# Six places instead of four for attention's exponentials, and a narrower layout of V

## The chip, the cores and the metric

The kernel runs on one core of a Trainium2 chip. The time is the device time of one execution in microseconds; the lower the better. Several executions are taken and their median is compared.

## The reference

The program is one forward pass over `x` of 2 sequences, 1024 tokens and width 128, in six residual steps: a small feed-forward, attention, the same feed-forward, a mixture of experts, a bidirectional Mamba block, the mixture of experts again. Each reads a layer norm of `x`. The change is in attention alone:

```python
qkv = x @ W_qkv.T + b_qkv            # 16 heads of 8
q, k = rope(q), rope(k)
scores = einsum('bhqd,bhkd->bhqk', q, k) / sqrt(8)
w = softmax(scores)                  # over 1024 keys
out = einsum('bhqk,bhkd->bhqd', w, v)
x = x + out
```

## The kernel before, in words

Everything stays in SBUF, and each stage is one program per engine, ordered by hand with semaphores. The first stage, `ffn_and_attention` (L747), runs the first feed-forward, attention, and, woven between attention's steps, the second feed-forward and the routing of the experts for both sequences. It ends near 325 us of the span. All engines meet at the end of its block (L763), and `moe_mamba_moe` follows.

Attention is cut into 16 blocks (`BLOCKS`, L648), eight per sequence. A block is one head of each group of four heads (`m`) and one half of the queries (512). A block has 16 steps (`UNITS`), one for each of 8 key tiles of 128 and each of 2 pairs of heads; step `w` of the 256 does:

- `scores` (L656), TensorE: two matmuls (one per head of the pair) of 128 keys by 512 queries into one of three PSUM places (`SB` = 3, each 128x1024 f32). In blocks 0 and 1 they are f32 with 32 rows (L677); from block 2 on, bf16 with 64 rows (L680), the f32 operands being split into bf16 parts and laid side by side by DMA. It waits until the exponential of step `w - 3` has freed the place.
- `exp` (L683), ScalarE: one ACTIVATE of 128x1024 from PSUM to one of `PB` = 4 places of `p` in SBUF (L687). It waits for its scores and, from step `PB` on, until the weighing of step `w - PB` has read the place (`summed`).
- `weigh` (L691), TensorE: two f32 matmuls (L703), weights V (128 keys by 32 columns), moving `p` (512 queries), into 32 rows of the PSUM bank `ps_av` for each group of heads. The 32 columns of V are: 8 values of the head, a 1 (so that the row sum of the softmax comes out of the same matmul) and zeros. For an even head the values stand at columns 0 to 7 and the 1 at 8; for an odd one at 16 to 23 and 24. So two heads one after the other can add into the same rows, each with zeros where the other's are.

The order on TensorE is written out in `ffn_and_attention` (from block 2 on), for even `w`, with `BEHIND` = 4:

```python
a.scores(pe, w)
a.weigh(pe, w - BEHIND)
a.weigh(pe, w - BEHIND + 1)
a.scores(pe, w + 1)
# then, at some steps, side work: a transpose, a projection, ...
```

In blocks 0 and 1 `scores(pe, w)` comes behind the two weighings. Side work stands after the scores of some steps: Q, K and V of the second sequence in blocks 4 and 5 (L361, L367), transposes of the norm (L1158) and of attention's output (L711), matmuls of the feed-forward (L1205, L1244) and of the routing (L1470). They use one PSUM bank in turn (`side`). When a turn of blocks closes, VectorE copies `ps_av` to `mixed` (L721), TensorE transposes it, and VectorE divides by the row sums and adds to `x` (`finish`, L714). At the first step of block 8 TensorE passes a branch on a flag (`shift_tensor`, L579), which is not taken with these inputs.

Other users of what the change touches: `fill` (L736), GpSimd, sets V to zero for one sequence (L739) and writes the ones (L743); `take_v` (L400), VectorE, adds the bias and writes V (L406); the first feed-forward (`FirstFfn`, L1256) keeps its 16 hidden values in `places`, which are the 8 halves of `p`, then the halves of `q`, `k_all` and `k`, and `rest`, all still unused at that time.

Of the kernel before, what the change touches and what calls it, by code (L numbers as in the profile page):

```python
# [16 lines left out]
P = 128  # L17
B, T, D = 2, 1024, 128
TILES = B * T // P
TPB = T // P  # L20
GROUP = 4
# [6 lines left out]
HEADS, HD = 16, 8  # L28
HG = 4
HGROUPS = HEADS // HG  # L30
# [83 lines left out]
class Core:  # L114
# [6 lines left out]
    def sb(self, name, shape, dt=F32, ctx=None):  # L121
        return (ctx or self.ctx).enter_context(self.nc.sbuf_tensor(name, shape, dt))

    def sem(self, name, ctx=None):

        s = self.nc.alloc_semaphore(name)
        if ctx is not None:
            self.stage_sems.append(s)
        return s
# [153 lines left out]
class Attention:  # L283
# [33 lines left out]
    def open(self, ctx):  # L317
        core, nc, name = self.core, self.core.nc, self.name
        sb = lambda n, shape, dt=F32: core.sb(f"{name}_{n}", shape, dt, ctx)
        sem = lambda n: core.sem(f"{name}_{n}", ctx)  # L320
        self.v = sb("v", [P, TILES, HEADS, 32])
        self.q, self.k_all, self.k = sb("q", [D, T]), sb("k_all", [D, T]), sb("k", [D, T])
        self.parts, self.rest = sb("parts", [D, 2, self.PARTS, T], BF16), sb("rest", [D, 2, GT])
        self.q_rows, self.k_rows = sb("q_rows", [P, 2, 2, T], BF16), sb("k_rows", [P, 2, 2, T], BF16)
        self.p = sb("p", [P, self.PB, 2, BANK])
        self.mixed = sb("mixed", [P, BANK])
        self.rden, self.scaled = sb("rden", [P, GROUP, HG, 2]), sb("scaled", [P, GROUP, HG, 2, HD])
        self.work = sb("work", [P, 7, GT])
        self.t_cos, self.t_sin = (self.work[:, 2 * i:2 * i + 2, :] for i in range(2))
        self.squares = self.mixed[:, 0:2 * D].rearrange("p (k d) -> p k d", k=2)  # L330
        self.b_squares, self.row_sums = sb("b_squares", [D, 2]), sb("row_sums", [D, 2])
        self.one = sb("one", [P, 1])
        self.head_sums, self.bounds, self.bound, self.flag = sb("head_sums", [1, 2 * HEADS]), sb("bounds", [1, HEADS]), sb("bound", [1, 1]), sb("flag", [1, 1], I32)
        self.top, self.minus_top = self.mixed[:, 2 * P:3 * P], self.mixed[:, 3 * P:4 * P]
        self.minus_parts = self.mixed[:, 0:2 * P].bitcast(BF16)[:, 0:self.PARTS * P].rearrange("p (j n) -> p j n", j=self.PARTS)
        self.marks_made = self.p[0:HD, 0, 0, :].bitcast(BF16)
        banks = ctx.enter_context(nc.psum_tensor(f"{name}_ps", [P, 8, BANK], F32))
        self.ps = banks
        self.ps_s, self.ps_av, self.ps_side = banks[:, 0:2 * self.SB, :].rearrange("p (s a) n -> p s a n", a=2), banks[:, 6, :], banks[:, 7:8, :]
        self.v_filled, self.masked_dve = sem("v_filled"), sem("masked_dve")  # L340
        self.qk_done, self.v_done, self.v_read, self.qk_read, self.rot_done = (sem(n) for n in ("qk_done", "v_done", "v_read", "qk_read", "rot_done"))
        self.masked_act, self.shift_in, self.stored = sem("masked_act"), sem("shift_in"), sem("stored")
        self.part0, self.rested, self.part1, self.part2 = (sem(n) for n in ("part0", "rested", "part1", "part2"))
        self.landed = [sem(f"landed{i}") for i in range(2)]
        self.squared, self.rows_summed, self.rows_done, self.heads_summed, self.heads_read, self.flagged = (
            sem(n) for n in ("squared", "rows_summed", "rows_done", "heads_summed", "heads_read", "flagged"))
        self.scored, self.exped, self.summed, self.av_read, self.turned, self.den_done, self.out_done, self.o_read = (
            sem(n) for n in ("scored", "exped", "summed", "av_read", "turned", "den_done", "out_done", "o_read"))
        of_both = {n: sem(f"shift_{n}") for n in ("turned", "negated")}
        self.shifting = [{**of_both, **{n: sem(f"shift{b}_{n}") for n in ("masked", "scored", "maxed", "own", "kept", "rows")}} for b in range(B)]  # L350
        self.registers = {}
# [48 lines left out]
    def take_v(self, dve, side, i):  # L400

        nc = self.core.nc
        dve.wait_ge(self.v_done, i + 1)
        dve.wait_ge(self.v_filled, 3 * (i // 2) + 3)
        for odd in range(2):
            ins = nc.vector.tensor_tensor(self.v[:, i * GROUP:(i + 1) * GROUP, odd::2, self.column(odd):self.column(odd) + HD],  # L406
                                          side.of(("v", i)).rearrange("p (j h d) -> p j h d", j=GROUP, h=HEADS)[:, :, odd::2, :],
                                          self.b_v[:].rearrange("p (h d) -> p h d", h=HEADS)[:, odd::2, :].unsqueeze(1).to_broadcast([P, GROUP, HEADS // 2, HD]),
                                          ALU.add)
        ins.then_inc(self.v_read, 1)  # L410

    @staticmethod
    def column(m):
        return 16 * (m % 2)

    def mask_first(self, act):
        self.core.landed(act, "head_mask")
# [220 lines left out]


    UNITS = 2 * TPB  # L640
    SB, PB = 3, 4
    BLOCKS = [(0, 0, 0, 0), (0, 0, 1, 0), (0, 1, 0, 1), (0, 1, 1, 1), (0, 2, 0, 2), (0, 3, 0, 3), (0, 2, 1, 2), (0, 3, 1, 3)]
    BLOCKS += [(1, 0, 0, 4), (1, 1, 0, 5), (1, 2, 0, 6), (1, 3, 0, 7), (1, 2, 1, 6), (1, 3, 1, 7), (1, 0, 1, 8), (1, 1, 1, 9)]
    TURNS = [(0,), (1,), (2,), (3,), (4, 5), (6, 7), (8, 9), (10, 11), (12, 13), (14, 15)]
# [46 lines left out]
    def weigh(self, pe, w):  # L691
        n, u = w // self.UNITS, w % self.UNITS
        b, m, half, _ = self.BLOCKS[n]
        kt, pair = u // 2, u % 2
        if u in (0, TPB):
            pe.wait_ge(self.v_read, 2 * b + u // TPB + 1)
        if u == 0:
            if n and self.opens(n):
                pe.wait_ge(self.av_read, self.turn_of(n))
        pe.wait_ge(self.exped, w + 1)  # L700
        for j in range(2):
            i = 2 * pair + j
            ins = self.core.nc.tensor.matmul(self.ps_av[32 * i:32 * i + 32, :], self.v[:, b * TPB + kt, HGROUPS * i + m, :],  # L703
                                             self.p[:, w % self.PB, j, :], start=(kt == 0 and self.opens(n)), stop=(kt == TPB - 1 and self.closes(n)))
        ins.then_inc(self.summed, 1)

# [29 lines left out]
    def fill(self, pool, b):  # L736

        nc, v = self.core.nc, self.v[:, b * TPB:(b + 1) * TPB, :, :]
        nc.gpsimd.memset(v, 0.0).then_inc(self.v_filled, 1)  # L739
        pool.wait_ge(self.v_filled, 3 * b + 1)  # L740
        for odd in range(2):
            one = self.column(odd) + HD
            nc.gpsimd.memset(v[:, :, odd::2, one:one + 1], 1.0).then_inc(self.v_filled, 1)  # L743
        pool.wait_ge(self.v_filled, 3 * b + 3)


# [1045 lines left out]
class Mamba:  # L1792
# [271 lines left out]
    def window(self, u, c, k):  # L2064

        di, b = self.UNITS[u]
        t0 = k if di == 0 else 2 * (TAPS - 1) - k
        return self.padded[:, c % 2, t0:t0 + T], self.taps[:, di, c, k:k + 1]
# [804 lines left out]
```

## Time and profile before

| | us |
|---|---|
| runs: 860.19, 863.32, 865.90; median | 863.32 |
| span of the profiled execution, first to last instruction | 852.2 |
| median less that span | 11.1 |
| first and last start of an exponential | 46.4, 318.6 |
| PE, ACT, DVE busy | 716.2, 543.8, 496.4 |

The page gives for the profiled execution only its span; what lies around it is taken as the 11.1 us by which the median of the runs is longer. PE is TensorE's matmuls, PEld its weight loads, ACT ScalarE, DVE VectorE, POOL GpSimd. An f32 matmul leaves two records (two passes), so one `weigh` has four and a bf16 `scores` two. Ends of matmuls are modelled: records of consecutive matmuls overlap, and the time that one takes of TensorE is read from start to start. "Idle before" of an instruction is the time in which its engine had nothing running, and behind the arrow stands what released it.

### The profile page before, as it was taken

The page shows a single profiled execution, that of the slowest core. Times are in us where ns is not written, and L with a number is a line of the kernel's source. Part 1 is how long each engine was busy: PE and PEld are TensorE (multiplying, and loading weights), DVE is VectorE, ACT ScalarE, POOL GpSimd, SP SyncE. Part 2 cuts the span into 40 slices and gives each one's busy share as a digit, 9 for nine tenths or more (in the row PEclk, how much of TensorE's full clock was granted, in tenths as well). Part 3 has the DMA queues.
Part 4 walks back from the last instruction along what each step waited for, and adds up shares of the span by engine and source line. Part 5 has one row for each costly group of instructions (what it writes and reads, how often), then busy time and mean ns, then how long its engine had stood idle before and what let it go on. Part 6 is the DMA issues. An engine that isn't in the chain of part 4 may idle for free. (4 is left out here: it accounts for less than half of the span.)

```text
span 852.2 us, 12981 instructions
## 1 busy us (share of the span) xinstructions
PE 716.2 (84%) x4016; PEld 373.4 (44%) x4016; DVE 496.4 (58%) x1453; ACT 543.8 (64%) x938; POOL 298.8 (35%) x328
## 2 busy tenths in 40 slices
PE   4799999989999997898779886778887768797995
PEld 1432222212222224565446454566566645564654
DVE  6778432204855747743437469798798847332352
ACT  5367997889998983644256684967877615342331
POOL 3090003301000434434323456444562732545342
PEclk9799999999999999999889988998999979998998
DMA  4046934521492211112212042112221311211313
GB/s 130 1 187 161 183 86 81 199 91 60 175 261 82 86 36 50 40 34 50 80 28 55 20 117 56 58 50 60 71 72 52 99 49 56 58 42 47 88 53 89
DMA packets 76410, 70.11 MB, mean 82 GB/s; under 512 B 9687, under 2 KB 60233, under 8 KB 76080
## 3 DMA queue, kind: packets, MB, share of 16 engines
q1 hardware_dynamic: 71024, 60.56, 26.6%
q0 software_dynamic: 5024, 8.54, 3.0%
q8 instruction: 36, 0.59, 0.3%
q14 instruction: 38, 0.31, 0.1%
q10 hardware_dynamic: 288, 0.10, 0.1%
HBM read 41.23 MB, written 29.02 MB: 82 GB/s over the span
## 5 line engine op out<-in xcount | busy, mean ns | idle before, releaser
L687 ACT ACTIVATE attn_p<-attn_ps 128x1024 f32<-128x1024 f32 x256 | 240.7, 1059 | 34.7 <-PE attn_ps L703 20.7
L1665 PE MATMUL ps_main<-moe_xsT,moe_w 128*128 128x320 f32 x384 | 131.0, 469 | 14.6 <-issue 9.1
L703 PE MATMUL attn_ps<-attn_p,attn_v 128*32 128x512 f32 x1024 | 137.5, 608 | 4.2 <-issue 4.0
L1675 ACT ACTIVATE moe_act_h<-ps_main 128x320 f32<-128x320 f32 (+1 forms) x128 | 55.1, 433 | 115.2 <-PE ps_main L1665 60.6
L1690 DVE TENSOR_TENSOR moe_hid<-moe_act_h,ps_main 128x320 f32<-128x320 f32 (+1 forms) x128 | 61.9, 485 | 110.8 <-ACT moe_act_h L1675 51.0
L1559 POOL DMA_INDIRECT moe_slots<-rows,moe_scatter_at x64 | 63.8, 997 | 97.8 <-DVE moe_scatter_at L1548 38.0
L680 PE MATMUL attn_ps<-attn_q_rows,attn_k_rows 64*128 64x512 bf16 x448 | 84.5, 388 | 11.5 <-ACT attn_p L687 7.7
L1665 PEld LDWEIGHTS ps_main<-moe_xsT,moe_w 128*128 128x128 f32 x384 | 70.7, 200 | 49.7 <-issue 29.5
L1695 PE MATMUL ps_main<-moe_hid,moe_w 128*128 128x320 f32 (+1 forms) x256 | 74.9, 458 | 5.1 <-DVE moe_hid L1690 3.7
L680 PEld LDWEIGHTS attn_ps<-attn_q_rows,attn_k_rows 64*128 64x128 bf16 x448 | 20.3, 93 | 134.2 <-ACT attn_p L687 119.6
L1765 POOL DMA_INDIRECT moe_rows<-moe_y,moe_dest x48 | 46.2, 962 | 78.6 <-ACT moe_y L1758 39.7
L2084 DVE SCALAR_TENSOR_TENSOR mb_act<-mb_padded,mb_taps,mb_act 128x1024 f32<-128x1024 f32 x48 | 67.1, 1407 | 2.9 <-ACT mb_act L2075 2.3
L1695 PEld LDWEIGHTS ps_main<-moe_hid,moe_w 128*128 128x128 f32 (+1 forms) x256 | 41.9, 192 | 34.7 <-issue 15.3
L1195 POOL TENSOR_TENSOR x_sb<-x_sb,bout_half 128x1024 f32<-128x1024 f32 (+1 forms) x4 | 7.3, 1837 | 104.7 <-DVE rows L1150 104.7
L2245 POOL TENSOR_TENSOR mb_z<-mb_y_in,mb_z 128x256 f32<-128x256 f32 x24 | 26.3, 1098 | 47.8 <-DVE mb_y_in L2236 33.0
L436 POOL TENSOR_SCALAR attn_parts<-attn_q 128x512 bf16<-128x512 f32 x4 | 2.5, 616 | 114.6 <-DVE attn_q L398 114.6
L2124 ACT ACTIVATE mb_e_seg<-mb_cums,mb_cum_col 128x128 f32<-128x128 f32 x128 | 40.5, 389 | 1.2 <-DMA mb_cums<-mb_cum_kept 1.2
L703 PEld LDWEIGHTS attn_ps<-attn_p,attn_v 128*32 128x32 f32 x1024 | 20.6, 108 | 42.5 <-issue 36.9
L2048 PE MATMUL ps_side<-norm_xT,mb_w_xbc 128*128 128x512 f32 x64 | 33.4, 641 | 5.5 <-DVE mb_ab L2017 5.5
L1765 POOL DMA_INDIRECT moe_rows<-mb_y,moe_dest x24 | 22.9, 955 | 38.8 <-ACT mb_y L1758 24.8
L2179 PE MATMUL ps_main<-mb_xw,mb_bs 128*128 128x256 f32 x56 | 20.0, 442 | 19.6 <-DVE mb_h L2202 12.8
L2156 DVE TENSOR_TENSOR mb_mt<-mb_e_seg,mb_gm 128x512 f32<-128x512 f32 x32 | 26.9, 840 | 15.6 <-ACT mb_e_seg L2131 9.5
(273 smaller groups left out, 1288.0 us busy)
## 6 DMA issues: line engine op xcount, KB each, us to landing
mb_cums<-mb_cum_kept SPq DMA_DIRECT2D x32, 256.0 KB
moe_slots<-zeros SPq DMA_DIRECT2D x4, 1380.0 KB, 14.0
attn_q_rows<-attn_q_parts SPq DMA_DIRECT2D x36, 128.0 KB
attn_k_rows<-attn_k_parts SPq DMA_DIRECT2D x36, 128.0 KB
moe_w<-in_w SPq DMA_DIRECT2D x3, 1536.0 KB, 11.6
moe_rows<-zeros SPq DMA_DIRECT2D x4, 1024.0 KB, 16.2
moe_back<-moe_rows SPq DMA_DIRECT2D x16, 256.0 KB, 4.0
mb_e_cum<-mb_e_cum_kept SPq DMA_DIRECT2D x56, 64.0 KB
```

Source lines behind the costliest of these rows:

```text
L680: ins = self.core.nc.tensor.matmul(into, self.k_rows[rows, ring, pair, keys], self.q_rows[rows, ring, pair, queries], start=True, stop=True)
L687: self.core.nc.scalar.activation(self.p[:, w % self.PB, :, :].rearrange("p a n -> p (a n)"), self.ps_s[:, w % self.SB, :, :].rearrange("p ...
L703: ins = self.core.nc.tensor.matmul(self.ps_av[32 * i:32 * i + 32, :], self.v[:, b * TPB + kt, HGROUPS * i + m, :], self.p[:, w % self.PB, ...
L1559: nc.gpsimd.indirect_dma_start(self.slots[r], bass.IndirectOffsetOnAxis(self.scatter_at[:, b, k, j:j + 1], 0), self.row_of[:, b * TPB + j, ...
L1665: self.core.nc.tensor.matmul(ps[:, w % 2, 0:CAP], wt[:, e, c * P:(c + 1) * P], self.xsT[:, u % 2, :], start=True, stop=True).then_inc(self ...
L1675: self.core.nc.scalar.activation(self.act_h[into, w % 2, :], self.ps_h1[rows, w % 2, 0:CAP], ACT.Silu).then_inc(self.silu_done, 1)
L1690: self.core.nc.vector.tensor_tensor(self.hid[rows, u % 2, c, :], self.act_h[rows, w % 2, :], bank[rows, w % 2, 0:CAP], ALU.mult)\
L1695: return self.core.nc.tensor.matmul(self.y_bank(u)[:, 0:CAP], self.w2[rows, u % E_, c, :], self.hid[rows, u % 2, c, :], start=start, stop= ...
L1765: self.core.nc.gpsimd.indirect_dma_start(self.rows[u // E_], bass.IndirectOffsetOnAxis(self.dest[0:n, u % self.DEST, s:s + 1], 0), self.y[ ...
L2048: self.core.nc.tensor.matmul(bank[:], weight, self.xT[:, t0:t0 + BANK], start=True, stop=True).then_inc(self.proj_done, 1)
L2084: ins = self.core.nc.vector.scalar_tensor_tensor(out, src, tap, out, ALU.mult, ALU.add)
L2124: ins = nc.scalar.activation(self.e_seg[:, g % 2, hh, :], self.cums[:, g % 2, hh, :], ACT.Relu, bias=self.cum[:, di, n, hh:hh + 1], scale= ...
```

## The change

`p` gets six places instead of four. V is kept for a pair of heads (even, odd) in 48 columns instead of 2 x 32: the even head at 0 to 8, the odd one at 32 to 40, zeros between; the even head's window is columns 0 to 31, the odd one's 16 to 47, so that they share 16 columns of zeros. What a window holds is what it held before. V shrinks from 32 to 24 KB a partition and `p` grows from 16 to 24 KB. `places` of the first feed-forward, which counts on `2 * a.PB`, now has 12 halves of `p` ahead of `q`, `k_all`, `k` and `rest`, so the values 8 to 11 move to `p`, 12 to 15 to `q` and `k_all`.

```diff
-        self.v = sb("v", [P, TILES, HEADS, 32])
+        self.v = sb("v", [P, TILES, HEADS // 2, self.PAIR])
...
-            ins = nc.vector.tensor_tensor(self.v[:, i * GROUP:(i + 1) * GROUP, odd::2, self.column(odd):self.column(odd) + HD],
+            ins = nc.vector.tensor_tensor(self.v[:, i * GROUP:(i + 1) * GROUP, :, self.column(odd):self.column(odd) + HD],
...
+    PAIR = 48
+
     @staticmethod
     def column(m):
-        return 16 * (m % 2)
+        return 32 * (m % 2)
+
+    @staticmethod
+    def window(m):
+        return slice(16 * (m % 2), 16 * (m % 2) + 32)
...
-    SB, PB = 3, 4
+    SB, PB = 3, 6
...
-            ins = self.core.nc.tensor.matmul(self.ps_av[32 * i:32 * i + 32, :], self.v[:, b * TPB + kt, HGROUPS * i + m, :],
+            ins = self.core.nc.tensor.matmul(self.ps_av[32 * i:32 * i + 32, :], self.v[:, b * TPB + kt, (HGROUPS * i + m) // 2, self.window(m)],
...
-            nc.gpsimd.memset(v[:, :, odd::2, one:one + 1], 1.0).then_inc(self.v_filled, 1)
+            nc.gpsimd.memset(v[:, :, :, one:one + 1], 1.0).then_inc(self.v_filled, 1)
```

## Rows read from the trace of the kernel before

**Rows 1.** The page: busy time (us, share of the span) and instructions of each engine.

```profile
PE 716.2 (84%) x4016; PEld 373.4 (44%) x4016; DVE 496.4 (58%) x1453; ACT 543.8 (64%) x938; POOL 298.8 (35%) x328
```

**Rows 2.** Busy time by stretches of 20 us, attention (us; then PEclk, DMA share, GB/s).

```profile
core 0: us, PE busy (x) PEld busy (x) DVE busy (x) ACT busy (x) POOL busy (x), PEclk, DMA share, GB/s
...
120.00:140.00 20.00, 19.65 (x122) 5.41 (x118) 6.58 (x12) 15.97 (x18) 3.87 (x5) 1.00 0.84 167
...
160.00:180.00 20.00, 18.75 (x136) 4.25 (x136) 1.21 (x3) 19.89 (x23) 1.80 (x2) 1.00 0.56 205
```

**Rows 3.** The exponential's line, L687: the start of what the view of one line gives.

```profile
L687 ACT ACTIVATE attn_p<-attn_ps x256: 1016/1032/1215, 46.4 to 318.6; 128x1024 f32<-128x1024 f32 x128
its engine sat idle before it (us, times) until:
  PE attn_ps L703: 20.7, 29
  PE attn_ps L677: 11.1, 11
```

**Rows 4.** Timeline of ACT, 84 to 320 us (start us, us, what, xcount [idle before <-releaser]).

```profile
124.56 1.94 ACT L687 ACTIVATE attn_p<-attn_ps 128x1024 f32<-128x1024 f32 x2 [0.21 <-PE attn_ps L703]
127.25 1.94 ACT L687 ACTIVATE attn_p<-attn_ps 128x1024 f32<-128x1024 f32 x2 [0.76 <-PE attn_ps L703]
...
132.64 1.94 ACT L687 ACTIVATE attn_p<-attn_ps 128x1024 f32<-128x1024 f32 x2 [0.76 <-PE attn_ps L703]
...
138.07 7.44 ACT L687 ACTIVATE attn_p<-attn_ps 128x1024 f32<-128x1024 f32 x8 [0.79 <-PE attn_ps L703]
...
156.88 29.65 ACT L687 ACTIVATE attn_p<-attn_ps 128x1024 f32<-128x1024 f32 x32 [0.79 <-PE attn_ps L703]
...
303.76 9.48 ACT L687 ACTIVATE attn_p<-attn_ps 128x1024 f32<-128x1024 f32 x10 [1.38 <-issue]
```

**Rows 5.** Timeline of PE, one pair of exponentials beside a projection.

```profile
131.16 0.39 PE L680 MATMUL attn_ps<-attn_q_rows,attn_k_rows 64*128 64x512 bf16 x2
131.48 1.06 PE L703 MATMUL attn_ps<-attn_p,attn_v 128*32 128x512 f32 x8
132.48 0.39 PE L680 MATMUL attn_ps<-attn_q_rows,attn_k_rows 64*128 64x512 bf16 x2
132.80 1.12 PE L361 MATMUL attn_ps<-norm_xT,attn_w 128*128 128x512 f32 x2
133.86 0.39 PE L680 MATMUL attn_ps<-attn_q_rows,attn_k_rows 64*128 64x512 bf16 x2
```

**Rows 6.** Timeline, two even steps in blocks 0 and 1: f32 scores and their exponentials.

```profile
53.68 0.88 PE L677 MATMUL attn_ps<-attn_q,attn_k 32*128 32x512 f32 x4
...
53.70 2.17 ACT L687 ACTIVATE attn_p<-attn_ps 128x1024 f32<-128x1024 f32 x2
...
72.30 0.71 PE L677 MATMUL attn_ps<-attn_q,attn_k 32*128 32x512 f32 x4
...
73.48 1.94 ACT L687 ACTIVATE attn_p<-attn_ps 128x1024 f32<-128x1024 f32 x2 [1.76 <-PE attn_ps L677]
```

**Rows 7.** Timeline of ACT, two short stands that lie alone.

```profile
161.42 2.20 ACT L687 ACTIVATE attn_p<-attn_ps 128x1024 f32<-128x1024 f32 x2
...
281.63 2.25 ACT L687 ACTIVATE attn_p<-attn_ps 128x1024 f32<-128x1024 f32 x2
```

**Rows 8.** Timeline, the step into batch 1 (block 8).

```profile
187.30 0.59 PE L680 MATMUL attn_ps<-attn_q_rows,attn_k_rows 64*128 64x512 bf16 x2 [2.67 <-ACT attn_p L687]
...
187.82 1.93 PE L703 MATMUL attn_ps<-attn_p,attn_v 128*32 128x512 f32 x8
...
189.69 1.04 PE L680 MATMUL attn_ps<-attn_q_rows,attn_k_rows 64*128 64x512 bf16 x4
189.85 3.03 ACT L687 ACTIVATE attn_p<-attn_ps 128x1024 f32<-128x1024 f32 x3 [3.31 <-PE attn_ps L703]
```

**Rows 9.** The page's costly groups: weight loads of the weighing.

```profile
L703 PEld LDWEIGHTS attn_ps<-attn_p,attn_v 128*32 128x32 f32 x1024 | 20.6, 108 | 42.5 <-issue 36.9
```

**Rows 10.** Timeline of POOL, the first microseconds.

```profile
1.62 3.51 POOL L739 MEMSET attn_v<- 128x4096 f32 x1
...
7.95 0.30 POOL L1278 TENSOR_SCALAR bout_half<-bout_sb 128x128 f32<-128x128 f32 x1 [2.45 <-DMA wout_sb<-in_wout]
```

**Rows 11.** Waits, 0 to 440 us: who waited for whom (us in total, times, longest).

```profile
POOL attn_parts L436 <- DVE attn_q L398: 114.6, 3, 70.3
```

**Rows 12.** Timeline, the last exponentials and the next stage's start.

```profile
317.68 1.96 ACT L687 ACTIVATE attn_p<-attn_ps 128x1024 f32<-128x1024 f32 x2
320.37 0.26 PE L1480 MATMUL attn_ps<-moe_picked,moe_tri 128*128 128x32 bf16 x4 [1.57 <-DVE moe_picked L1524]
...
325.24 0.61 PE L1593 MATMUL ps_main<-ident,moe_first_slots 128*128 128x128 f32 x3 [2.11 <-PEq L763]
```

**Rows 13.** Busy time by stretches after attention (columns as in rows 2).

```profile
325.00:430.00 105.00, 89.62 (x352) 55.94 (x353) 59.39 (x221) 46.74 (x110) 43.68 (x50) 0.95 0.19 52
430.00:530.00 100.00, 80.58 (x353) 50.56 (x351) 63.81 (x127) 64.94 (x140) 46.15 (x44) 0.90 0.21 58
...
sum 527.00, PE 428.93 PEld 289.68 DVE 324.28 ACT 284.48 POOL 236.02; mean PE 85.78 PEld 57.94 DVE 64.86 ACT 56.90 POOL 47.20
```

## The prediction, made before the changed kernel was run

> **What bounds the kernel now.** I read the page first. TensorE is the busiest engine over the whole span, 716.2 us, and ScalarE next with 543.8 [rows 1]; that average says little about attention. Cut into stretches, attention is bound now by the one, now by the other: from 120 to 140 us TensorE is busy 19.65 of 20 us and ScalarE 15.97; from 160 to 180 us ScalarE is busy 19.89 and TensorE 18.75 [rows 2]. Then the view of the line of the exponentials: 256 of them, started from 46.4 to 318.6 us, and ScalarE sat idle before them for 20.7 us, 29 times, until a weighing (L703) ended, and for 11.1 us until f32 scores of blocks 0 and 1 ended [rows 3]. The first number is what the change aims at: with four places the exponential of an even step w waits for the weighing of w - 4, which stands on TensorE right behind the scores of w. With six it waits for w - 6, which stands ahead of them.
>
> The timelines give the prices. Where nothing holds ScalarE, 32 exponentials take 29.65 us [rows 4], that is (29.65 - 1.2) / 31 = 0.918 us each, the last one's own length of 1.2 taken off [rows 3]. Beside a projection TensorE works back to back: scores 131.16, two weighings 131.48, scores 132.48, projection 132.80, next scores 133.86 [rows 5]. So a pair of steps costs TensorE 0.32 + 1.00 + 0.32 = 1.64 us, under ScalarE's 1.83, and with the projection's 1.06 it costs 2.70, over it. ScalarE's pairs there start 2.69 us apart (124.56 to 127.25) with 0.76 us idle ahead of each [rows 4]: TensorE sets that pace, and the missing place only says at which point of the pair ScalarE stands still.
>
> **Part 1: six places.** The change takes one wait away and adds no instruction. Take the pair whose scores start at 131.16. Its exponentials now start at 132.64, 1.48 us later, and at 132.64 + (1.94 - 1.02) = 133.56, 2.40 us later [rows 4, 5], the 1.02 us being a single one [rows 3]. Without the wait the even one is due when its scores are: these take 0.39 us [rows 5], and from their end to the exponential I take 0.47 us, from an even step of block 1 whose four score records end at 72.30 + 0.71 = 73.01 and whose exponential starts at 73.48 [rows 6]. So the even one starts 0.86 us after its scores started, 0.62 earlier than now. The odd one gains less. Its scores stand behind both weighings on TensorE, 0.32 + 1.00 = 1.32 us after the even ones, so it can't start before 1.32 + 0.86 = 2.18 us, where it now starts at 2.40. Gain 0.22 us; the other 0.40 of the even one's 0.62 is a new stand ahead of the odd one, released by L680.
>
> In a run of such pairs this 0.22 comes once. The pairs follow each other at TensorE's 2.70 us with either number of places. At the end of the run ScalarE sets the pace again, 0.22 us ahead, TensorE follows it (its scores wait for the place that step w - 3 frees), and the next run begins 0.22 us earlier. So I count runs, not waits. The 29 waits and the one of 1.38 us put down to issue at 303.76 [rows 3, 4] fall into 16 runs, taking waits less than 3.6 us apart as one: those that begin at 92, 99, 109, 117, 125 (six waits), 146 (five), 190, 196, 204, 214, 228, 245, 258, 293, 304 and 314 us. 16 x 0.22 = 3.5 us. Two short stands lie alone besides, at 162.6 and 282.9 us, where two exponentials start 2.20 - 1.02 = 1.18 and 1.23 us apart instead of 0.92 [rows 7]; they are of the same kind, 0.2 each: 3.9. The run at 190 gains nothing: there TensorE's pair of weighings took 1.87 us instead of 1.00, the odd step's scores started at 189.69, and the odd exponential, 0.92 behind that of 189.85, already stood at these [rows 8]. Sum 3.7 us.
>
> Blocks 0 and 1 gain nothing: their scores stand behind the weighings, and ScalarE waits for L677 [rows 3]. The 2.67 us in which TensorE stood before block 8 [rows 8] is put down to ScalarE, whose exponential had ended 2.6 us before; it is the passage of the branch, and stays.
>
> The unknown is the 0.47 us. No bf16 row shows it at full clock. The longest it can be is 0.69, the shortest distance from the end of bf16 scores to an exponential seen there (132.87 to 133.56, paced by ScalarE itself) [rows 4, 5]: then the odd one is due at 2.40, and the gain is nothing. The shortest is 0.29 us, in block 0: scores ended at 53.68 + 0.88 = 54.56, and the exponential started at 53.70 + 2.17 - 1.02 = 54.85 [rows 6]. Then the gain is 0.22 + 0.18 = 0.40 us, in 17 places 6.8. I take 0.47: the same two engines and semaphores, and a matmul of records that follow without a stand, as the bf16 ones do.
>
> **Part 2: the V windows.** 1024 weight loads of 128x32 at 108 ns [rows 9], as many as before, of as many columns; they start while the matmuls before them run. I cost them at nothing. If reading at a stride of 192 bytes doubled them, about 0.1 us would show twice in a pair of steps. That is the slower rival below. It can't be below nothing, the rows of the array being loaded are the same.
>
> **Part 3: the smaller fill, the places of the first feed-forward.** The memset of 4096 elements took 3.51 us, and 3072 should take 2.63. The first ends into a wait of POOL for a load that lasts 2.45 us longer [rows 10], the second, near 61 us, into one of up to 70 us for the rope of the second sequence [rows 11]. Worth nothing on either path; without the cover the first would give 0.9. The first feed-forward writes the same instructions to other addresses: nothing.
>
> **What carries it to the end.** After the last exponential the routing of the second sequence is a chain (ScalarE, VectorE, TensorE at 320.37, VectorE), and the engines meet before 325.24 [rows 12]; that chain starts at the exponentials and moves with them. The rest, 527 us, begins at this meeting and is as before. So the span should be 852.2 - 3.7 = 848.5 us. The median of the runs is 11.1 above the profiled span, so the time is 863.3 - 3.7 = 859.6 us.
>
> **A rule against the change.** The rows above leave TensorE as the bound in the very pairs in which ScalarE waits. The Trainium skill, TensorE: Matmul & The Clock Gate, section HAM oscillation, reports of a matmul kernel already kept busy that adding double buffers in PSUM "gave no further gain". Carried over to `p` it would make the sum 0 and the time 863.3, against 859.6 by the rows; the rows show neither buffer count at work, so it stands as a rival's backing only.
>
> **The rivals.**
> - No change, 863.3 us: the 0.22 us never reaches the odd exponential, because its release takes 0.69, not 0.47. For it: every odd bf16 exponential shown stands so. Against it: there ScalarE is always the later one. The rule just told would also land here. Chance 0.2.
> - All of the 20.7 us come back: 863.3 - 20.7 = 842.6. For it: the view of the waits names L703 29 times [rows 3]. Against it: TensorE's starts leave no room [rows 5]. Chance 0.04.
> - Slower: the weight loads of the windows. If each group of eight showed 0.1 us twice, the pair goes from 1.64 to 1.84, level with ScalarE's 1.83, which is the point from which it decides everywhere. Some 45 pairs are paced by TensorE (16 of blocks 0 and 1, the 29 that wait): 45 x 0.2 = 9.0, less 3.7, is 5.3 slower, 868.6 us. Against it: the loads stand beside matmuls, and their engine idled 42.5 us ahead of them [rows 9]. Chance 0.06.
> - The clock of what follows: TensorE's granted clock is 0.95 in one stretch and 0.90 in the next [rows 13], and all starts move by 3.7 us against what sets it. A mean clock 0.01 higher or lower over the 429 us of TensorE work is 4.3 us: 855.3 or 863.9. Chance 0.14, split evenly.
>
> The forecast holds the remaining 0.56.
>
> **Numbers.** The forecast's own gain is 3.7 with its bounds 0 and 6.8, so 856.5 to 863.3; the median of three runs itself moves by a microsecond or two (the runs before lie between 860.19 and 865.90). Widened for that and for half of the clock's cases: 855.0 to 864.5. A measurement of this kernel tells about 1%, 8.6 us. Faster than 854.7: the second rival, and the good half of the clock's case where it adds to noise, 0.06. Slower than 871.9: a part of the slower rival and of noise, 0.03. Within 1%: 0.91.
>
> **What would show it.** In the profile of the changed kernel the idle time before L687 released by L703 falls from 20.7 to near nothing, and a new one released by L680, and to a smaller part still ahead of even steps, takes some 16 us of it. In the projections of blocks 4 and 5 TensorE's scores still start 2.70 us apart, but ScalarE's pair of exponentials is split, 1.3 us apart instead of 0.92. The last exponential starts at 314.9 instead of 318.6. L739 takes 2.6 us. The stages behind are as long as before. Wrong would be: scores to exponential longer than 0.6 us; a weighing pair over 1.00 us from start to start; a last exponential before 312 or after 317.

## The result, and the profile after

The changed kernel takes 852.55 us in the median of 4 runs (851.65 to 853.35); the kernel before, with one run more, 861.76 us (856.23 to 865.90). The ratio is 0.9897, interval 0.9853 to 0.994: 9.2 us or 1.0% faster, where 3.7 us were forecast. The time lies under the low end of the range, 855.0.

The view of the exponentials' line in the changed kernel, which answers to [rows 3] (L693 is the old L687, L709 the old L703, L686 the old L680, L683 the old L677):

```profile
L693 ACT ACTIVATE attn_p<-attn_ps x256: 1017/1050/1327, 44.8 to 308.7; 128x1024 f32<-128x1024 f32 x128
its engine sat idle before it (us, times) until:
  PE attn_ps L686: 14.1, 35
  PE attn_ps L683: 10.7, 11
  issue: 0.6, 2
```

The waits for the weighing are gone, and 14.1 of their 20.7 us have turned into waits for bf16 scores. From the first to the last start the exponentials took 318.6 - 46.4 = 272.2 us and now take 308.7 - 44.8 = 263.9, so attention is 8.3 us shorter in this pair of profiles. The pair beside a projection that answers to [rows 4, 5], timeline of TensorE and ScalarE:

```profile
125.02 0.39 PE L686 MATMUL attn_ps<-attn_q_rows,attn_k_rows 64*128 64x512 bf16 x2
125.34 1.06 PE L709 MATMUL attn_ps<-attn_p,attn_v 128*32 128x512 f32 x8
125.45 1.02 ACT L693 ACTIVATE attn_p<-attn_ps 128x1024 f32<-128x1024 f32 x1 [0.35 <-PE attn_ps L686]
126.34 0.39 PE L686 MATMUL attn_ps<-attn_q_rows,attn_k_rows 64*128 64x512 bf16 x2
126.66 1.13 PE L361 MATMUL attn_ps<-norm_xT,attn_w 128*128 128x512 f32 x2
126.77 1.02 ACT L693 ACTIVATE attn_p<-attn_ps 128x1024 f32<-128x1024 f32 x1 [0.29 <-PE attn_ps L686]
127.72 0.39 PE L686 MATMUL attn_ps<-attn_q_rows,attn_k_rows 64*128 64x512 bf16 x2
```

TensorE's starts are as before: 0.32, 1.00, 0.32, 1.06, together 2.70 us. The exponentials are split as forecast, 126.77 - 125.45 = 1.32 us apart. But each starts 0.43 us after its scores started, 0.04 after the end that the profile models for them (125.02 + 0.39 = 125.41), and not 0.86 and 0.47. That is the number on which the forecast rested: 0.47 where 0.04 was the case. All 39 stands of over 0.05 us that ScalarE has from block 2 on look so.

The shorter memset and the pass on VectorE beside it. The kernel before, timeline near 64 us:

```profile
61.25 3.51 POOL L739 MEMSET attn_v<- 128x4096 f32 x1
...
64.15 0.89 DVE L1229 TENSOR_SCALAR attn_work<-attn_work,w_sb,minus_b 128x512 f32<-128x512 f32 x1
```

and the changed kernel:

```profile
59.62 2.66 POOL L745 MEMSET attn_v<- 128x3072 f32 x1
...
62.51 0.55 DVE L1235 TENSOR_SCALAR attn_work<-attn_work,w_sb,minus_b 128x512 f32<-128x512 f32 x1
```

The memset takes 2.66 us as forecast, and ends before VectorE's pass begins, which is 0.34 us shorter. The prediction had asked who waits for the memset, not who works beside it.

The step into block 8, TensorE's clock. Before (columns as in rows 2; the third number from the end is the granted clock):

```profile
186.00:188.00 2.00, 0.70 (x6) 0.30 (x10) 0.00 (x0) 0.53 (x1) 0.00 (x0) 0.84 0.48 142
188.00:190.00 2.00, 2.00 (x10) 0.15 (x7) 0.00 (x0) 0.15 (x1) 0.00 (x0) 0.50 0.43 126
```

After:

```profile
182.00:184.00 2.00, 1.39 (x12) 0.35 (x14) 0.00 (x0) 0.96 (x1) 0.00 (x0) 1.00 0.52 175
184.00:186.00 2.00, 2.00 (x16) 0.31 (x16) 0.38 (x1) 1.70 (x3) 0.00 (x0) 1.00 0.51 171
```

In the profile of before the clock fell from 2.4 to 1.2 GHz after TensorE's stand of 2.67 us there; in the one of after it did not, though the stand was 2.72 us:

```profile
182.61 0.39 PE L686 MATMUL attn_ps<-attn_q_rows,attn_k_rows 64*128 64x512 bf16 x2 [2.72 <-ACT attn_p L693]
```

One more number can't be compared as it seems. The spans are 852.2 and 851.6 us, nearly equal, with attention 8.3 us shorter. The profiled execution of the kernel before was a quick one in the stages behind: from the last exponential to the end 852.2 - 318.6 = 533.6 us against 851.6 - 308.7 = 542.9. The changed kernel's result lists both numbers of one execution, a span of 851.6 and a time of 853.35, so 1.75 us lie around a span, not 11.1. By that the profiled execution of before took about 854 us, 8 under its median.

### The profile page after: what moved, and what is told of

Same layout as the page of the kernel before. It is cut to its first block and busy times, and to the rows that moved or that the text cites. A ratio compares the mean times of both kernels' runs of the same rounds, so it can differ in the third digit from the quotient of the medians.

```text
span 851.6 us, 12979 instructions
## 1 busy us (share of the span) xinstructions
PE 722.3 (85%) x4016; PEld 380.0 (45%) x4016; DVE 496.2 (58%) x1453; ACT 544.1 (64%) x938; POOL 298.6 (35%) x328
## 5 line engine op out<-in xcount | busy, mean ns | idle before, releaser
L693 ACT ACTIVATE attn_p<-attn_ps 128x1024 f32<-128x1024 f32 x256 | 241.0, 1082 | 26.2 <-PE attn_ps L686 14.1
L1671 PE MATMUL ps_main<-moe_xsT,moe_w 128*128 128x320 f32 x384 | 136.5, 485 | 18.1 <-DVE moe_hid L1696 11.8
L709 PE MATMUL attn_ps<-attn_p,attn_v 128*32 128x512 f32 x1024 | 136.4, 604 | 5.7 <-issue 5.6
L1671 PEld LDWEIGHTS ps_main<-moe_xsT,moe_w 128*128 128x128 f32 x384 | 74.0, 209 | 54.7 <-issue 35.7
L686 PE MATMUL attn_ps<-attn_q_rows,attn_k_rows 64*128 64x512 bf16 x448 | 79.8, 385 | 6.1 <-ACT attn_p L693 3.5
L686 PEld LDWEIGHTS attn_ps<-attn_q_rows,attn_k_rows 64*128 64x128 bf16 x448 | 19.0, 93 | 122.0 <-ACT attn_p L693 95.4
L709 PEld LDWEIGHTS attn_ps<-attn_p,attn_v 128*32 128x32 f32 x1024 | 20.4, 107 | 46.6 <-issue 34.3
```

Source lines behind the costliest of these rows:

```text
L686: ins = self.core.nc.tensor.matmul(into, self.k_rows[rows, ring, pair, keys], self.q_rows[rows, ring, pair, queries], start=True, stop=True)
L693: self.core.nc.scalar.activation(self.p[:, w % self.PB, :, :].rearrange("p a n -> p (a n)"), self.ps_s[:, w % self.SB, :, :].rearrange("p ...
L1671: self.core.nc.tensor.matmul(ps[:, w % 2, 0:CAP], wt[:, e, c * P:(c + 1) * P], self.xsT[:, u % 2, :], start=True, stop=True).then_inc(self ...
```

## The experiments

The lengths below are from the start of the first exponential to that of the last, in each run's own profile; they leave out the stages before and behind, whose length varied between executions (behind: 520 to 543 us over all profiles). Steps are compared by the starts of their exponentials, each counted from the first one. Where an experiment is marked "one execution" it was run once, and only its length is used. Three chips were used after the first result; the kernel before took 840.74, 839.56 and (one run) 849.39 us on them.

**The changed kernel again** (`r1_same`), no edit.

> The changed kernel once more, as the measure for the other runs. Both theories: 852 to 854 us, exponentials from first to last start in 264 us, against 272 us in the kernel before. If the 9 us lie in attention (8.3 us by the two profiles) the kernel before comes out near 861 again; if they were luck of the stages behind, the two draw together to 4 us.

831.42 us against 840.74, ratio 0.987 (0.9811 to 0.9929), 9.3 us. Length 309.1 - 45.1 = 264.0 us:

```profile
L693 ACT ACTIVATE attn_p<-attn_ps x256: 1016/1053/1355, 45.1 to 309.1; 128x1024 f32<-128x1024 f32 x128
```

The gain repeats, in the time and in the length of attention. Two places differ between these two profiles of one kernel, and both matter for what follows. The start of step 128 comes 0.43 us later here, behind a stand of 3.15 us on TensorE, with the clock at 1.00. And before step 240, where TensorE waits for VectorE's part of the feed-forward, ScalarE stands 0.68 us here and 1.04 in the first profile. So differences of 0.4 us at these two places are differences between executions.

**V's layout alone** (`r2_v_only`).

```diff
-    SB, PB = 3, 6
+    SB, PB = 3, 4
```

> V in 48 columns a pair, but four places. Theory (the lost wait is the gain): first to last exponential about 272 us less 0.35 us, because the shorter memset lets go of VectorE earlier near 65 us; time within 1 us of the kernel before. Rival (the layout of V, weight loads or addresses, is the gain): 264 us, time 853.

840.00 us, ratio 0.9989 (0.9959 to 1.0018). Length 270.6 us:

```profile
L693 ACT ACTIVATE attn_p<-attn_ps x256: 1017/1042/1215, 44.9 to 315.4; 128x1024 f32<-128x1024 f32 x128
its engine sat idle before it (us, times) until:
  PE attn_ps L709: 21.6, 30
```

1.6 us shorter than before, not 0.35. The clock did not fall in this one at block 8 (1.00 from 178 to 194 us), and 1.2 of the remaining 1.3 us come there, at steps 128 to 136. Against the changed kernel, which differs from it in the number of places alone and whose clock did not fall there either, it is 6.7 us longer (6.6 against `r1_same`).

**Six places, the wait kept** (`r3_wait_kept`).

```diff
-        if w >= self.PB:
-            act.wait_ge(self.summed, w - self.PB + 1)
+        if w >= 4:
+            act.wait_ge(self.summed, w - 4 + 1)
```

> The whole change, but the exponential of step w still waits for the weighing of step w - 4: six places, no gain from them. Theory: as the kernel with V alone, first to last exponential 271.8 us. Rival (places at other addresses, values of the first feed-forward in other tiles): 264 us.

842.05 us, ratio 0.999 (0.9966 to 1.0014), length 271.9:

```profile
L693 ACT ACTIVATE attn_p<-attn_ps x256: 1017/1032/1215, 45.4 to 317.3; 128x1024 f32<-128x1024 f32 x128
its engine sat idle before it (us, times) until:
  PE attn_ps L709: 22.9, 31
```

As expected to 0.1 us, with the clock at 0.50 near block 8, as in the profile of before. It differs from the changed kernel in this one wait, and is as slow as the kernel before. The wait is the gain; places, addresses and windows are not.

**Six places beside the old V** (`r4_six_old_v`) does not fit: SBUF is 7,072 bytes a partition short. The 8 KB that the narrower V frees are what the two places take.

**Five places** (`r5_five`).

```diff
-    SB, PB = 3, 6
+    SB, PB = 3, 5
```

> Five places instead of six. Theory: the even step's wait for w - 4 is all that stood in the way, and the weighing of w - 5 is issued ahead of the scores of w - 1, so it has always ended: 264 us from first to last exponential, as with six, time as the changed kernel. Rival (the depth of the ring itself counts, each place by half): 267 to 268 us, time half way to the kernel before.

833.12 us, ratio 0.9923 (0.9899 to 0.9947), length 264.9. Up to step 127 it keeps step with the changed kernel to 0.02 us. At steps 128 and 129, where the clock fell in this execution (0.72, then 0.50), it falls 1.4 us behind, and before step 240 it regains 0.4, as `r1_same` does. So five do as well as six in attention. The time's ratio and that of `r1_same` overlap.

**The second memset out of the way** (`r6_fill_late`), one execution.

```diff
                 first_ffn.base(pool)
+                pool.wait_ge(a.exped, 3 * UNITS)
                 a.fill(pool, 1)
```

> The changed kernel, but GpSimd sets V of the second sequence to zero only after block 2, when VectorE has no L1235 to run. Theory (GpSimd's memset holds up VectorE's two-operand-scalar pass): the first L1235 of the second feed-forward takes 0.55 us in every case, as it does now, and the exponentials of steps 16 to 20 keep their 5.59 us; nothing is gained over the changed kernel, which had already got out of the memset's way. Rival (more contention is left): steps 0 to 32 shorter than 39.8 us by up to 0.3 us.

Length 263.5 us, steps 0 to 32 in 39.80 as before it, steps 16 to 20 in 5.59. Nothing was left there to gain.

**The same move in the kernel before** (`r9_old_fill_late`), one execution, the same edit.

> The kernel before with one move: GpSimd zeroes V of the second sequence after block 2. Theory (the memset on GpSimd holds up VectorE, which holds up the weighing of step 16): the first L1229 of the second feed-forward takes 0.55 us instead of 0.89, and steps 16 to 20 take 5.59 us instead of 5.94. Rival (the 0.35 us has another source, such as where V lies): 0.89 and 5.94 stay.

Timeline of VectorE:

```profile
62.71 0.55 DVE L1230 TENSOR_SCALAR attn_work<-attn_work,w_sb,minus_b 128x512 f32<-128x512 f32 x1
```

0.55 us instead of 0.89, and steps 16 to 20 took 5.59 us instead of 5.94. With the old V and four places this settles it: the memset held up VectorE's pass, that pass held up the copy L721, and the weighing of step 16 waits for the copy. Over the whole of attention the run was no shorter (273.1 us): by step 132 the clock, which was at 0.50 for longer at block 8, had cost it 0.9 us more than in the profile of before, and the stand before step 240 was 0.3 us longer (1.71 against 1.38). The rule is in the Trainium skill, SBUF — State Buffer, section Who interferes with whom: VectorE's `tensor_scalar` can take the pair of ports that GpSimd uses, and then the one has to wait for the other. This trace agrees in kind: 0.34 us lost, with the two overlapping by 0.61.

**Scores first in blocks 0 and 1** (`r7_scores_first`).

```diff
-                        if n >= 2 and w < TOTAL:
+                        if n >= 0 and w < TOTAL:
                             a.scores(pe, w)
...
-                        if n < 2:
+                        if n < 0:
                             a.scores(pe, w)
```

> The changed kernel with the scores of the even step ahead of the weighings in blocks 0 and 1 too. Theory: pairs there take 2.07 to 2.24 us of which TensorE's own work is 0.53 + 0.54 + 1.00 = 2.07, so at most 0.17 us in each second pair comes back, 1 to 1.5 us of the 39.8 us of steps 0 to 32; time 1 us shorter, too little to tell in the rounds. Rival: steps 0 to 32 as long or longer, because the first weighings then wait behind scores that wait for a place.

836.67 us, ratio 0.9962 (0.9928 to 0.9996); steps 0 to 32 took 43.1 us instead of 39.8. A miss for the theory. The rival had the direction, but not the reason: it is the matmuls that became longer. Its timeline:

```profile
59.10 1.13 PE L683 MATMUL attn_ps<-attn_q,attn_k 32*128 32x512 f32 x4
60.16 0.66 PE L1164 MATMUL attn_ps<-ident,rows 128*128 128x128 f32 x4
...
60.75 1.13 PE L683 MATMUL attn_ps<-attn_q,attn_k 32*128 32x512 f32 x4
61.80 1.07 PE L709 MATMUL attn_ps<-attn_p,attn_v 128*32 128x512 f32 x8
```

The f32 scores of one step take 1.06 us from start to start when they stand alone (59.10 to 60.16). In the kernel before two steps in a row take 1.08:

```profile
72.30 1.14 PE L677 MATMUL attn_ps<-attn_q,attn_k 32*128 32x512 f32 x8
73.38 0.65 PE L711 MATMUL attn_ps<-ident,attn_mixed 128*128 128x128 f32 x4
```

The two steps use different 32-row strips of the array. By these times they run side by side when they are adjacent, and do not with other matmuls between them. The edit puts the side work of blocks 0 and 1 between the two steps of four pairs (behind 55.41, 59.10, 62.80 and 73.52 us).

**No branch ahead of block 8** (`r8_no_branch`). It leaves out the shift of the scores for large weights on TensorE.

```diff
-                    if (n, u) == (LAST + 1, 0):
-                        a.shift_tensor(pe, 1)
```

> The changed kernel without TensorE's branch at the step into block 8. It leaves out the shift of the scores for large weights, which these inputs never take. Theory: ScalarE's stand of 1.24 us at step 128 goes, first to last exponential 262.5 to 263 us, time 1 us shorter; TensorE's clock stays at its upper level there. Rival (the stand at step 128 is a wait for the rows' DMA): 264 us as before.

826.14 us, ratio 0.9817 (0.9765 to 0.9869), the fastest of all, though it is not the whole kernel. Length 306.8 - 45.6 = 261.2 us:

```profile
L693 ACT ACTIVATE attn_p<-attn_ps x256: 1018/1059/1418, 45.6 to 306.8; 128x1024 f32<-128x1024 f32 x128
its engine sat idle before it (us, times) until:
  PE attn_ps L686: 12.6, 34
```

2.7 us less than the changed kernel: 2.1 by step 129, 2.3 by step 136, and the last 0.36 before step 240, where `r1_same` and others gain it with the branch too. TensorE's stand ahead of block 8 shrinks from 2.72 to 0.22 us:

```profile
180.93 0.39 PE L686 MATMUL attn_ps<-attn_q_rows,attn_k_rows 64*128 64x512 bf16 x2 [0.22 <-ACT attn_p L693]
```

So a branch that is never taken costs 2.3 us here, without any fall of the clock: TensorE can be at most three places of scores ahead of ScalarE, and they run out while it stands. That is more than the expected 1.24, since the even exponential comes 1.7 us earlier and the odd one behind it gains another 0.4.

**Odd steps keep the wait** (`r10_odd_kept`), one execution.

```diff
-        if w >= self.PB:
-            act.wait_ge(self.summed, w - self.PB + 1)
+        back = 4 if w % 2 else self.PB
+        if w >= back:
+            act.wait_ge(self.summed, w - back + 1)
```

> The changed kernel, but exponentials of odd steps still wait for the weighing of w - 4; those of even steps for w - 6. Theory (only the even steps' wait ever bound): 264 us from first to last exponential, as the changed kernel. Rival (the odd ones gain of themselves): 266 us or more.

Length 266.5 us, over the rival's 266. But up to step 127 it is within 0.01 us of the changed kernel, 2.6 us come between steps 128 and 131, where the clock was at 0.50 for 6.8 us, and behind that nothing more is lost:

```profile
182.00:184.00 2.00, 0.33 (x2) 0.14 (x2) 0.00 (x0) 0.59 (x1) 0.00 (x0) 0.71 0.37 99
184.00:186.00 2.00, 2.00 (x10) 0.20 (x8) 0.00 (x0) 1.02 (x1) 0.00 (x0) 0.50 0.53 184
186.00:188.00 2.00, 2.00 (x16) 0.34 (x12) 0.00 (x0) 1.28 (x2) 0.00 (x0) 0.50 0.50 174
188.00:190.00 2.00, 2.00 (x16) 0.31 (x12) 0.69 (x1) 1.10 (x2) 0.00 (x0) 0.59 0.20 75
```

Outside that place the odd steps' wait cost nothing. Whether it does where the clock is low this run can't tell.

**The wait kept, no branch** (`r11_kept_no_branch`), one execution; the edits of `r3_wait_kept` and `r8_no_branch` together.

> The changed kernel with the wait for w - 4 kept on all steps, and without TensorE's branch ahead of block 8 (it leaves out the shift for large weights, not taken here). Beside the run without the branch and without the wait (261.2 us) it gives the wait's worth where TensorE's clock can't fall at block 8. Theory: 6.6 us, that is 267.8 us. Rival (a part of the gain is the clock's and the branch's): 264 to 266 us.

```profile
L693 ACT ACTIVATE attn_p<-attn_ps x256: 1014/1042/1217, 45.2 to 313.5; 128x1024 f32<-128x1024 f32 x128
its engine sat idle before it (us, times) until:
  PE attn_ps L709: 19.1, 29
```

Length 268.4 us. Against the 261.2 of `r8_no_branch`, where the clock did not fall either, the wait alone is worth 7.1 us (268.37 - 261.23). Some 0.3 of this may be the execution's: the stand before step 240 is 1.70 us here, and 1.38 in three other profiles with the wait. The pair with the branch, `r2_v_only` and the changed kernel, gave 6.7. So the wait is worth 6.6 to 7.1 us; the expected 6.6 is at the low end.

## Why the prediction was wrong

**The mechanism held.** TensorE sets the pace beside side work, 2.70 us a pair with either number of places; the even exponential moves by more than the odd one; only the odd one's gain stays, and never more than once for each run of such pairs (from step 70 to step 80, six waits, the distance between the kernels with and without the wait grows by 0.40 us in all); L686 takes the place of L709 as the releaser. All of it stands in the profile after, and `r3_wait_kept` shows that nothing but the wait did it.

**The term that was mis-sized is the gain of a run, 0.22 us.** It rested on 0.47 us from the end of scores to the exponential, read from f32 scores of block 1 [rows 6], because no bf16 row showed it. In bf16 it is 0.04 us. So the odd exponential is due 1.32 + 0.43 = 1.75 us after the even scores started, not 2.18, against 2.40 before: 0.65 us where the run's first stand is long enough, as between steps 83 and 91 of `r8_no_branch` and `r11_kept_no_branch`, whose distance grows from 2.10 to 2.76 us. Where the exponentials at the head of the run start 1.31 us apart, the run can gain no more than ScalarE stood, 1.31 - 0.92 = 0.4 us. Between these two kernels four of the 16 runs (at 146, 214, 245 and 304 us) gain 0.61 to 0.65 us, eight gain 0.34 to 0.45, the one at 190 gains 0.2, and those at 204, 228 and 293 nothing, which no run explains; single short stands make up the rest. The 17 places of the forecast and the measured 6.6 to 7.1 us make 0.4 us each on the average, about twice the 0.22. The prediction's own sign of being wrong came with it: a last exponential before 312 us (308.7). The bound of 6.8 us was near this by luck: its 0.29 us came from f32 ends too. Both f32 rows say the same when read from the start of the scores, 54.85 - 53.68 = 1.17 and 73.48 - 72.30 = 1.18 us [rows 6]; only the modelled ends differ. The distance from a modelled end to a waiting engine is no constant (0.04, 0.29 and 0.46 us in this kernel); it held for one shape and type, and starts should have been compared instead, with the bound open downward.

**"Worth nothing on either path"** failed for the second memset. POOL's own wait hid it, but not from VectorE: 0.35 us, shown by `r9_old_fill_late` in the kernel before.

**"The 2.67 us ... stays"** was right for the stand (2.72 after), and the loss behind it was booked as part of the kernel. It was that execution's. The length of before is 272.18, of the changed kernel 263.91: 8.27 us. `r2_v_only` lies between them: from before to it 1.6 us, of which 0.35 is the memset's and 1.3 comes at block 8, where its clock did not fall; from it to the changed kernel 6.7 us, the wait's. `r2_v_only` and `r3_wait_kept`, with the same wait, lie 1.4 us apart at block 8, with and without the fall, which bears the 1.3 out. These are single profiles, and each term is good to some 0.4 us. Whether the change makes the fall rarer is open: with the wait on all steps it came in 3 of 4 profiles that had the branch, otherwise in 2 of 6.

**The sum's frame.** The 11.1 us taken for what lies around the span were 1.75; the median of before was itself drawn from runs 10 us apart. Neither enters the difference of 9.2 us that the four and four runs show, and the repeat gives 9.3. The wait and the memset together are worth 6.9 to 7.5 us of it. The other two stay open, within the intervals (0.9853 to 0.994 is 5 to 13 us): a rarer fall of the clock would be a part; the first exponential starts 1.6 us earlier in the profile after (clock back to 2.4 GHz a little sooner, at 37.7 instead of 40.6 us), which may be an execution's matter; and the stages behind vary by more.

**The rivals.** "No change" fell: one more place is worth 6.6 to 7.1 us, 0.8%. The remark of the Trainium skill that backed it is on PSUM buffers of another kernel, and did not carry over to `p`. The weight loads of the windows cost nothing: weighings start 1.00 us before what follows, as before, and their loads took 107 ns. A load reads 32 columns that lie side by side in either layout, so the stride of 192 bytes that this rival named is none within a load. "All of the 20.7" fell too, 14.1 of it stayed. The clock of the stages behind is not what made the gain, most of which stands in attention's length; the mean granted clock was lower in the profile after, 0.939 against 0.950.

## What to carry to other kernels

A wait named by the profile says what came last, not what it is worth. Write down the next thing that would be late on both engines and subtract starts; here about a third of the 20.7 us was to be had, because TensorE was the next limit. Before that subtraction rests on a release time, find it for the same data type and shape, or leave the bound open. And of an instruction that is made shorter, ask who runs beside it, not only who waits for it.

## What the runs showed of the hardware

- An exponential that waits for bf16 scores starts 0.43 us after their start, 0.04 us after their modelled end (36 to 42 ns at all 39 such waits of the changed kernel); with the clock at 1.2 GHz these were 0.65 and 0.04 us (`r5_five`, steps 128 and 129). Behind f32 scores it starts 1.17 us after their start, 0.29 or 0.46 us behind the modelled end. The modelled ends are not on one scale.
- A GpSimd memset of 128x4096 f32 held up a VectorE `tensor_scalar` of 128x512 f32 that began 0.6 us before its end: 0.89 us instead of 0.55.
- TensorE stood for 2.7 to 3.1 us at the branch, and its clock fell to 1.2 GHz near the end of this stand in 5 of 10 profiles that had the branch, for 3 to 7 us, with four, five and six places, and in none of the 2 without it (stand 0.22 us). The fall cost 1.0 to 2.6 us each time, the stand itself 2.3.
- Two f32 score steps of 32 rows, in different strips, took 1.08 us together when adjacent, and 1.06 us each with other matmuls between them (`r7_scores_first`).
